# A recurrence of 256 steps: the copy of each state moves from ScalarE to VectorE, and two waits change place

## What is computed

```python
def step(h, xt):
    m = jnp.concatenate([xt, h], axis=-1) @ weight + bias
    c = jnp.tanh(m[:, units:])
    g = jax.nn.sigmoid(m[:, :units] + 1.0)
    h_new = g * h + (1.0 - g) * c
    return (h_new, h_new)
```

## Time and profile before

| | us |
|---|---|
| median of 3 runs | 491.91 |
| lowest and highest run | 491.33, 492.35 |
| the profiled execution's own time | 492.14 |
| its span, first to last instruction | 490.3 |
| start of the first and of the last state scan | 15.3, 324.4 |

### The profile page before, as it was taken

The page is one execution under the profiler, slowest core; times in us unless marked ns, Lnnn a source line. Parts: engine busy times, 40 slices in busy tenths (PEclk is TensorE's granted clock), DMA queues, the critical chain, the costliest instruction groups (busy, mean ns, idle before and its releaser), DMA issues.

```text
span 490.3 us, 11840 instructions
## 1 busy us (share of the span) xinstructions
PE 361.2 (74%) x3776; PEld 216.1 (44%) x3776; DVE 326.7 (67%) x1685; ACT 327.3 (67%) x1275; POOL 78.9 (16%) x152
## 2 busy tenths in 40 slices
PE   2876789877945676854688797897868979786832
PEld 1533455444623443533444454453544536455510
DVE  5456455576688776687767677664482457889893
ACT  2456665666767856766867776764668898972952
POOL 6000000011100011100011100004130032356580
PEclk9999999999999999999999999996758998997877
DMA  7100920002000000000000000000000000000002
GB/s 177 50 3 6 217 40 3 0 2 44 3 1 2 1 2 1 1 2 1 2 2 1 2 2 2 1 2 1 3 3 2 3 1 3 2 1 1 23 0 64
DMA packets 9120, 8.29 MB, mean 17 GB/s; under 512 B 1282, under 2 KB 7700, under 8 KB 9060
## 3 DMA queue, kind: packets, MB, share of 16 engines
q1 hardware_dynamic: 8964, 7.29, 6.5%
q0 software_dynamic: 96, 0.26, 0.2%
HBM read 6.47 MB, written 1.08 MB: 15 GB/s over the span
## 4 chain that ended last, share of the span: by engine, by line
PE 38%; DVE 27%; ACT 20%; issue 10%; POOL 1%; DMA 1%; DVEq 1%; SPq 0%; ACTq 0%; POOLq 0%
PE zb L836 9%; DVE state L1603 7%; ACT sets L1318 5%; ACT sets L1302 3%; PE tb L964 3%; DVE guessed L1603 3%; PE firsts L1135 3%; PE tb L774 3%; PE zb L813 2%; PE firsts L1020 2%; ACT prd L1460 2%; PE tb L935 2%; PE zb L1115 2%; ACT prd L1440 2%; ACT qs L1403 2%
## 5 line engine op out<-in xcount | busy, mean ns | idle before, releaser
L1302 ACT ACTIVATE sets<-zb 128x32 f32<-128x32 f32 x479 | 103.6, 225 | 63.2 <-PE zb L836 49.4
L1603 DVE TENSOR_TENSOR_SCAN state<-sets 128x32 f32<-128x32 f32 x256 | 57.3, 224 | 61.8 <-ACT sets L1302 56.4
L836 PE MATMUL zb<-rest,whh 128*128 128x8 f16 x480 | 47.4, 169 | 62.5 <-DVE rest L1624 56.4
L836 PEld LDWEIGHTS zb<-rest,whh 128*128 128x128 f16 x480 | 33.6, 106 | 123.1 <-ACT sets L1302 96.2
L1318 ACT ACTIVATE sets<-state 128x32 f32<-128x32 f32 x255 | 59.2, 232 | 28.4 <-DVE state L1603 16.1
L1603 DVE TENSOR_TENSOR_SCAN guessed<-sets 128x32 f16<-128x32 f32 x255 | 57.4, 225 | 27.6 <-ACT sets L1302 2.9
L836 PE MATMUL zb<-guessed,whh 128*128 128x8 f16 x960 | 64.6, 173 | 8.6 <-DVE guessed L1603 0.4
L836 PEld LDWEIGHTS zb<-guessed,whh 128*128 128x128 f16 x960 | 44.4, 107 | 28.0 <-DVE guessed L1603 0.6
L1624 DVE TENSOR_TENSOR rest<-state,guessed 128x8 f16<-128x8 f32 x255 | 42.6, 167 | 9.0 <-DVE state L1603 0.2
L1460 ACT ACTIVATE prd<-zb 128x640 f32<-128x640 f32 x64 | 41.9, 710 | 5.8 <-PE zb L1115 5.1
L630 POOL TENSOR_TENSOR stat<-mv 128x4 f32<-128x4 f32 x4 | 0.8, 208 | 239.8 <-DVE mv L1723 239.8
(11 more groups left out here) (370 smaller groups left out, 690.3 us busy)
## 6 DMA issues: line engine op xcount, KB each, us to landing
mod<-ada_rows SPq DMA_DIRECT2D x4, 768.0 KB, 12.5
resid<-in_x_dram SPq DMA_DIRECT2D x6, 128.0 KB, 3.6
ffz<-shift_rows SPq DMA_DIRECT2D x4, 131.0 KB, 3.6
out_dram<-state SPq DMA_DIRECT2D x8, 64.0 KB, 2.1
out_dram<-early SPq DMA_DIRECT2D x8, 64.0 KB, 2.1
yy<-in_L_cond_w_ada_dram SPq DMA_DIRECT2D x1, 384.0 KB
early<-in_L_cond_weight_dram SPq DMA_DIRECT2D x2, 128.0 KB
resid<-in_x_dram POOLq DMA_DIRECT2D x2, 128.0 KB, 3.4
```

The costliest lines, as they stand in the source:

```text
L836: return pe.matmul(bank[:, 256 * k + i:256 * k + i + NB], whh[:, half, k, :], h, start=False, stop=False, skip_group_check=True)
L1302: return act.activation(view(sets[:, n, 3:4], [39, 2], [38, 2], [4, NB]), view(bank[:, i:i + 1], [256, 2], [0, 2], [1, NB]), ACT.Tanh, sca ...
L1603: return dve.tensor_tensor_scan(dst, *scan_terms(n), 0.0, ALU.mult, ALU.add)
```

## The change

```diff
@@ TensorE, step(t)
+                pe.wait_ge(lo_ready, t + 1)
                 if t < STEPS - 1:
                     pe.wait_ge(guess_in, t + 1)
-                pe.wait_ge(lo_ready, t + 1)
                 z_part(t, 0, 0, rest[:, :])
                 z_part(t, 1, 0, rest[:, :]).then_inc(full_z, 1)
@@ ScalarE, step(t)
                 tanhs(t, 0).then_inc(tanh_in, 1)
                 if t + 1 < STEPS - 1:
                     guess(t + 1)
-                if t < STEPS - 1:
-                    act.wait_ge(h_ready, t + 1)
-                    act.activation(copies_of_h(0), view(h_row(t)[:, 3:4], [0, 2], [4, NB], [0, 2]),
-                                   ACT.Copy).then_inc(h_copied, 1)
@@ VectorE, step(t)
-                if t < STEPS - 1:
-                    dve.wait_ge(hi_ready, t + 2)
-                else:
+                dve.wait_ge(tanh_in, t + 1)
+                if t == STEPS - 1:
                     dve.wait_ge(h_copied, t)
-                dve.wait_ge(tanh_in, t + 1)
                 scan(h_row(t), 0).then_inc(h_ready, 1)
                 if t < STEPS - 1:
                     dve.wait_ge(h_ready, t + 1)
                     dve.tensor_tensor(rest[:, :], view(h_row(t)[:, 3:4], [4, NB]),
                                       guessed_h(t), ALU.subtract).then_inc(lo_ready, 1)
+                    dve.tensor_copy(copies_of_h(0), view(h_row(t)[:, 3:4], [0, 2], [4, NB], [0, 2]))\
+                       .then_inc(h_copied, 1)
                 if t + 1 < STEPS - 1:
                     guess(t + 1)
```

## The result

The changed kernel takes 466.82 us (median of 4 runs, 466.5 to 467.71) where the kernel before takes 491.62 beside it (490.97 to 492.35). The ratio is 0.950, with a 95% interval of 0.948 to 0.952. The forecast was 467.0. The profiled execution has a span of 465.3 us, 25.0 less than before.

A forecast was written before the change was run, and what follows sets the result against it. The prediction took single recurrence steps, a chain across engines, as the bound. Gains over 255 distances summed to 26.4 us, less 1.4, leaving 25.0: from 492.14 to 467.1, stated as 467.0 us after a median correction, range 460 to 482.

The forecast's parts named there:

- What bounds a step: In the recurrence, late signals on TensorE and VectorE pass through an extra sequencer wait, costing 0.06 and 0.07 us per step.
- the bare step: Recurrence step with no side work in its way; forecast to go from 1.13 to 1.00 us.
- The copy's price: On VectorE, the copy lasts 0.18 us, starting 0.08 behind rest's start; the guess's scan comes 0.02 later, at 0.55.
- ScalarE: In the recurrence, its side work starts at 0.26, not 0.40, after the state scan; 32 distances give 7.1 us less.
- the bare loop: Recurrence chain of state scan, rest, two matmuls and tanh, without side work: from 1.13 to 1.00 us per step.
- The bare loop's 98 distances: Of 255 distances between state scans in the recurrence, 98 limited by this chain alone: 13.0 us less.
- the guess's loop: In the recurrence: copy, guess's scan, four matmuls, its tanh; 2.00 us over two steps, so 1.00 per step.
- The 1.4 taken off for waits of side work: In the recurrence, half of TensorE's 3.0 us waiting for ScalarE's exponentials, subtracted from the 26.4 us gain.
- Rival D: In the recurrence, side work keeps its distance in time, so its gains become new waits: 479 us, chance 0.14.
- rival B: On VectorE, the copy waits for rest to drain but lasts 0.18; guess's scan at 0.64: 482 us, chance 0.11.
- The stage behind the recurrence: The work after the recurrence, forecast to keep its instructions, their order and its 166 us.

The follow-up runs named there:

- the two single waits: Two runs against the kernel before, copy left on ScalarE: TensorE's two waits swapped, 483.13 us; VectorE's hi_ready wait before the state scan removed, 476.77 us.
- two copies: Changed kernel plus a second copy of the same size on VectorE, into an unread buffer, ahead of the real one: 480.76 us.

## Why the prediction was right, and where it was off

**What bounds a step.** Right. That the early wait sat on the work and the late one on the sequencer was read from two rows without any experiment; two runs that changed nothing but waits moved the bare step by 0.06 to 0.07 each, as the prediction had it.

**The copy's price.** Right in size and place: 0.176 for 0.18, start 0.08 behind rest, guess at 0.55. It was called cheap because VectorE stood idle there. That holds against ScalarE's copy, which was waited for just as long. It is not free: without any copy the kernel is 20 us faster.

**ScalarE.** Right, with the step a little shorter than forecast. In the changed kernel the two steps with the side work of the earlier trace rows last 1.09 and 1.01 us (1.13 to 1.17 and the bare loop were forecast):

```profile
140.00 0.22 DVE L1599 TENSOR_TENSOR_SCAN state<-sets 128x32 f32<-128x32 f32 x1
140.13 0.23 ACT L1302 ACTIVATE sets<-zb 128x32 f32<-128x32 f32 x1 [0.18 <-PE zb L836]
140.23 0.71 ACT L1399 ACTIVATE qs<-yy 128x256 f16<-128x256 f32 x2
140.84 0.52 ACT L1302 ACTIVATE sets<-zb 128x32 f32<-128x32 f32 x2
141.09 0.23 DVE L1599 TENSOR_TENSOR_SCAN state<-sets 128x32 f32<-128x32 f32 x1
```

The side work starts right behind the guess's tanh, 0.23 behind the state scan, not 0.40.

**The bare loop's 98 distances.** Mis-sized: 100.5 for 98.0. The prediction said that the guess's loop is "just level with the bare loop" and then let it cost nothing. What was left out lies on TensorE, most of it in side work between the guess's matmuls and the next load for rest. A load with a free way starts 0.053 us behind rest; of the 255 loads, 55 start more than 0.065 behind it, all but two of them with side work right ahead. With no copy, so with an early guess, it is 17, and the same 98 distances take 97.8. With both waits changed and the copy left on ScalarE it is 53, so the 0.03 by which the move delays the guess is not what brings most of these. What the move does bring is the alternation of bare steps, which average 1.004 by it, against 1.00 in that run.

**The 1.4 taken off for waits of side work.** Right in size by chance, wrong in its reason. TensorE's waits for exponentials in the recurrence did not grow: 1.1 us in 3 waits, against the 3.0 in 6 of the earlier trace rows. What was lost is the term above. Rival D, in so far as it rests on these waits, falls with that, and rival B with the starts of the copies.

**The stage behind the recurrence.** It was to keep its 166 us and has 165.3. In the ten experiments it lasts 164 to 166, so 1 to 2 us of the gain of the two single waits lie there and not in the recurrence. Why it moves was not tried. In those two runs TensorE's granted clock there was 0.86 of full speed on average, a mean of its two levels (1.2 and 2.4 GHz), against 0.84 before, and TensorE was busy for 123 us instead of 126; but the run with no copy has 165.9 at 0.83 and that with two copies 164.6 at 0.83, so the clock alone does not order them.

## What to carry to other kernels

Of two waits in front of one instruction, the one that ends last should ride on the instruction itself, which here was the first of the two in the program; read from the trace which wait has a row of its own, and whether it is the late one. Before moving a small operation off an engine, ask what it holds back in its queue: here the copy's wait for the state held ScalarE's side work, and the move paid only in the steps that had any. When two loops come out level, count neither as free.

## What was not expected of the hardware

The number of elements hardly matters for a copy of this size on VectorE. Right behind rest, 16 elements per partition took 0.169 us and 32 took 0.176; the second copy of 16, behind the guess's scan, took 0.150. So half the elements save 7 to 26 ns of 176, while the next instruction could start 0.08 to 0.09 us behind the start of the one ahead. The Trainium skill, page "VectorE: DVE Perf Modes", section "Mode 2×_2P — use both read ports for one tensor", has fp32 copies within SBUF at two elements per cycle. At the page's 0.96 GHz that is 8 ns for 16 elements (an estimate; 17 at one per cycle): the 7 ns in the same place agree with it, the 26 ns to the copy in the other place do not, so no run here settles the rate.
